# Where the turned probabilities are copied: between the two row maxima on VectorE and between the two exponentials on ScalarE

## The reference, cut to what matters

```python
h = _layernorm(x, axis=-1) * (1 + ca) + sa
q = _l2norm(q) * q_scale          # q, k, v = projections of h, 16 heads of 64
k = _l2norm(k) * k_scale
attn = jnp.einsum('bhid,bhjd->bhij', q, k) * DH ** (-0.5)
attn = jax.nn.softmax(attn, axis=-1)
out = jnp.einsum('bhij,bhjd->bhid', attn, v)
x = x + ga * (out @ Wo.T + bo)    # then layernorm, router, experts
```

## Time and profile before

| | us |
|---|---|
| median of 3 runs | 1300.74 |
| lowest and highest | 1300.59, 1301.45 |
| the profiled execution | 1305.93 |
| its span, first to last instruction | 1304.2 |

### The profile page before, as it was taken

The page is one execution under the profiler, slowest core; times in us unless marked ns, Lnnn a source line. Parts: engine busy times, 40 slices in busy tenths (PEclk is TensorE's granted clock), DMA queues, the critical chain, the costliest instruction groups (busy, mean ns, idle before and its releaser), DMA issues. The chain is left out here.

```text
span 1304.2 us, 28717 instructions
## 1 busy us (share of the span) xinstructions
PE 1240.5 (95%) x9690; PEld 819.9 (63%) x9690; DVE 995.3 (76%) x2049; ACT 967.2 (74%) x2065; POOL 831.5 (64%) x1654
## 2 busy tenths in 40 slices
PE   4899999999999999999999999999998498999997
PEld 4556666666666666666666666666664276788886
DVE  3678778887887887888878878877877776577776
ACT  4677778777778777777778787877775286788886
POOL 2666677767767676777677677866774185344443
PEclk8799999999999999999999999999999699899999
DMA  6000000000000000000000000000000200446441
GB/s 158 2 1 2 1 2 2 2 2 1 2 2 1 2 2 1 2 2 2 2 1 2 2 2 2 1 2 2 1 2 1 67 1 23 102 100 109 100 106 46
DMA packets 36610, 27.99 MB, mean 21 GB/s; under 512 B 8832, under 2 KB 34688, under 8 KB 36480
## 3 DMA queue, kind: packets, MB, share of 16 engines
q1 hardware_dynamic: 35296, 25.92, 8.8%
q10 hardware_dynamic: 1184, 0.40, 0.1%
HBM read 24.09 MB, written 2.23 MB: 20 GB/s over the span
## 5 line engine op out<-in xcount | busy, mean ns | idle before, releaser
L881 ACT ACTIVATE probs<-bank,neg_max 128x512 f32<-128x512 f32 x512 | 347.2, 683 | 216.6 <-DVE neg_max L1013 213.7
L1013 DVE TENSOR_REDUCE neg_max<-bank 128x1 f32<-128x512 f32 x512 | 329.5, 685 | 140.5 <-PE bank L677 138.4
L717 PE MATMUL bank<-probsT,qkv 128*64 128x512 f32 x1024 | 276.8, 620 | 1.3 <-DVE oT L1030 0.8
L677 PE MATMUL bank<-operands 64*128 64x512 f32 x1536 | 249.2, 429 | 2.4 <-ACT probs L881 1.9
L693 PEld LDWEIGHTS T<-ident,probs 64*128 64x128 f32 x4096 | 168.9, 139 | 50.9 <-issue 25.6
L693 PE MATMUL T<-ident,probs 64*128 64x64 f32 x4096 | 172.4, 223 | 5.3 <-issue 3.7
L647 PEld LDWEIGHTS bank<-operands,hT_h 128*128 128x128 f32 x254 | 48.1, 189 | 199.0 <-issue 196.2
L677 PEld LDWEIGHTS bank<-operands 64*128 64x128 f32 x1536 | 125.5, 186 | 64.2 <-issue 42.1
L1197 POOL TENSOR_TENSOR sq<-qkv 128x256 f32<-128x256 f32 x252 | 150.1, 614 | 15.5 <-ACT qkv L860 15.4
L1019 DVE COPY probsT<-T 128x1024 f32<-128x1024 f32 x128 | 155.5, 1215 | 1.5 <-PE T L693 1.5
L1803 POOL TENSOR_TENSOR hid_l<-act_out,hid_h 128x512 fp32r<-128x512 f32 x64 | 83.1, 1298 | 110.0 <-ACT hid_h L1705 110.0
(11 more groups left out here) (259 smaller groups left out, 2371.9 us busy)
## 6 DMA issues: line engine op xcount, KB each, us to landing
probsT<-gate_scratch SPq DMA_DIRECT2D x64, 256.0 KB, 4.7
out<-x_all SPq DMA_DIRECT2D x8, 256.0 KB, 4.6
probsT<-in_L_ffn_fc_w SPq DMA_DIRECT2D x1, 1024.0 KB, 8.9
raw<-in_L_attn_Wq SPq DMA_DIRECT2D x1, 512.0 KB, 4.9
raw<-in_L_attn_Wk SPq DMA_DIRECT2D x1, 512.0 KB, 7.6
raw<-in_L_attn_Wv SPq DMA_DIRECT2D x1, 512.0 KB, 8.8
raw_o<-in_L_attn_Wo SPq DMA_DIRECT2D x1, 512.0 KB, 8.3
route<-in_L_ffn_sh_w SPq DMA_DIRECT2D x2, 256.0 KB, 5.6
```

What stands on the lines that cost most here:

```text
L677: last = nc.tensor.matmul(s_bank(hp, 2 * pair + head)[:], own[rows, q, toks], own[rows, k], start=((q, k) == (QH, KH)), stop=(q == QL))
L717: last = nc.tensor.matmul(O_BANK[rows, :], qkv[:, hp % 4, j, cols], probsT[:, hp % 2, head, j], start=(j == 0), stop=(j == NT - 1), skip_g ...
L881: nc.scalar.activation(probs[:, i % 4], s_bank(hp, i)[:], ACT.Exp, bias=neg_max[:, i:i + 1], accum_out=row_sum[:, hp % 2, i:i + 1]).then_i ...
L1013: nc.vector.reduce_max(neg_max[:, i:i + 1], s_bank(hp, i)[:], AX.X, negate=True).then_inc(max_done, 1)
```

## The change

The same instructions run; two copies in each slot change their place in their engine's order. On VectorE, in pair steps 0 and 2, the copy moves from behind the second maximum (and behind `low_q`) to between the two maxima. On ScalarE, in pair steps 1 and 3, the copy moves from behind the second exponential to between the two exponentials. TensorE's and GpSimd's order is the same.

```diff
@@ ScalarE, slot
                             exponentials(u, hp, 2 * pair)
-                            exponentials(u, hp, 2 * pair + 1)
                             if pair == 1 and earlier >= 1:
                                 copy_transposed(u - 1, hp - 1, 3)
                             if pair == 3:
                                 copy_transposed(u, hp, 1)
+                            exponentials(u, hp, 2 * pair + 1)
@@ VectorE, slot
                             row_max(u, hp, 2 * pair)
+                            if pair == 0 and earlier >= 1:
+                                copy_transposed(u - 1, hp - 1, 2)
+                            if pair == 2:
+                                copy_transposed(u, hp, 0)
                             row_max(u, hp, 2 * pair + 1)
                             if pair == 2 and with_next(b, hp, 1):
                                 low_q(u + 1, hp + 1)
                             if pair == 3 and with_next(b, hp, 1):
                                 low_k(u + 1, hp + 1)
                             if pair == 0 and hp == YT_HP and not is_const(b, 0):
                                 dve.wait_ge(x1_done, b)
-                            if pair == 0 and earlier >= 1:
-                                copy_transposed(u - 1, hp - 1, 2)
-                            if pair == 2:
-                                copy_transposed(u, hp, 0)
```

## The result

The changed kernel takes 1390.37 us (median of 4 runs, 1386.61 to 1392.84) against 1300.81 of before (1300.59 to 1301.45): a ratio of 1.0678, 95% interval 1.0654 to 1.0702, so slower by 6.8%. Its profiled execution took 1388.67 around a span of 1386.8.

The account below looks back on a forecast made before the run. TensorE's own work was taken to bound the slots, so VectorE or ScalarE edits could mainly lose by making it wait. 69.8 + 20.2 + 1 = +91 us on 1300.7 gave 1392, range 1368 to 1404.

Parts of the forecast that it names:

- +1: Behind the last slot: the last exponential comes 0.91 us later and the chain there is serial, +1 us.
- Term one: VectorE, pair step 2: the copy makes `low_q` and the turn of k 1.14 us later in 63 slots, +69.8 us.
- `low_q` without spare time: VectorE to TensorE, pair step 2: `transpose_k` starts 0.12 to 0.15 us behind `low_q`, about the signal between engines.
- The 0.29 that hp 3 had spare: Pair step 2 of hp 3: TensorE turns 0.44 us after `low_q` ends, so 0.29 is spare, 2.0 less in all.
- Term two: ScalarE, pair steps 1 and 3: a unit's last exponential comes 0.91 us later, delaying later scores in some slots, +20.2 us.
- The copy of pair step 0 at nothing: VectorE, pair step 0: the copy delays only the second maximum and its exponential by 1.14 us, no cost by itself.
- tenths that a spare of 1.01 holds: ScalarE, pair steps 0 and 1: later second exponential pushes other work back some tenths, within 1.01 us spare.
- Term one alone: Rival: the delay of the sums' inversion is absorbed, leaving only the pair step 2 loss, 1371 us; chance 8%.
- The copy never waited for the turn: Rival, VectorE pair step 2: the copy waits for TensorE's late turn, adding 13 us, 1405; chance 7%.
- The rival wasn't empty: Rival: TensorE's idle time lowers its granted clock in a tenth of the slots' time, up to +100, 1490 us; chance 4%.

Follow-up runs that it names:

- VectorE's pair step 2 alone: Kernel before with only VectorE's copy of pair step 2 moved between the two maxima: 1370.66 us against 1303.84, ratio 1.0524.
- pair step 3 undone: Changed kernel with ScalarE's copy of pair step 3 put back behind the second exponential: 1371.63 us, ratio 1.0530 to the kernel before.
- three of the runs above: Kernel before with ScalarE's two copies moved, 1324.91 us; changed kernel with VectorE's pair step 2 copy put back, 1326.63, or `low_q` ahead of that copy, 1380.45.
- the kernel with low_q ahead: Changed kernel with `low_q` put between the first maximum and the copy of pair step 2: 1380.45 us against 1304.95 of the kernel before, ratio 1.0585.
- the two runs with low_q ahead: In pair step 2 first maximum, `low_q`, copy, second maximum: in the changed kernel 1380.45 us; in the kernel before, for that step only, 1323.27.
- the split not late: Kernel before with GpSimd's split of an attention output in hp 0 and hp 3 not put behind the squares: span 1306.2 us, single execution.

## Why the prediction was right

**The sum.** Forecast 1392, measured 1390.4. That it is this close is partly luck. In the profiled executions the slots took 85.6 more, where my two terms make 90, and what lies behind the start of the last slot took 313.7 instead of 316.4, where I had counted +1; the spans differ by 82.6, the medians by 89.6. The kernel before ran at 1300.8 beside the changed one and at 1301.8 to 1305.0 beside the other runs. The four runs of the changed kernel go from 1386.6 to 1392.8 as their mean granted clock goes from 0.981 to 0.971. In the profiled one (0.977) batch 2 has the full clock, and the page's slices are below it only at the start and behind the slots; so a few us there are the clock's and not the change's.

**Term one (69.8)** measured 70.4 as a part of its own (VectorE's pair step 2 alone), 66.3 with all but pair step 3 moved, and 68.0 as TensorE's wait in the changed kernel (1.8 before). The step by which it was made, `low_q` without spare time, held in each slot, the same 0.12 behind. The 0.29 that hp 3 had spare came out in the changed kernel (4.78 less 3.90 is 0.88), but it stood on something that I hadn't looked at. TensorE was late in that slot because the turn waited for ScalarE's copy of pair step 1. With that copy moved, the changed kernel's step is 4.78 as in every slot; with it in its old place, VectorE's copy waited for the late turn, and nothing was spare (5.01). In hp 5 I missed as much: its step was 3.87 before and the loss 0.91.

**Term two (20.2)** measured 19.3 (with pair step 3 undone against the changed kernel), 22.8 alone, of which about 1.5 is the fall of the clock. In batch 0 hp 1 to hp 4 lost 1.08, 0.82, 0.92 and 0.83 at pair step 0, where I had 0.91 for each. In a later batch it is 1.9 to 2.1, where I had 2.45. Slot by slot: hp 3 lost 0.80 at pair step 0, as forecast; hp 1 lost 0.40 and 0.30 where I had 0.55 and 0.24; hp 4 lost 0.37 where I had 0.86; hp 5 lost 0.17, for which I had no row. The size of hp 4 is the term's largest error. In the kernel before, timeline of hp 1 and hp 4, GpSimd beside VectorE:

```profile
536.95 1.03 POOL L1213 TENSOR_TENSOR inv_wide<-inv_sum,consts 128x512 f32<-128x512 f32 x1
...
537.67 0.34 DVE L995 TENSOR_SCALAR ss<-ss 128x16 f32<-128x16 f32 x1
...
581.98 1.04 POOL L1213 TENSOR_TENSOR inv_wide<-inv_sum,consts 128x512 f32<-128x512 f32 x1
...
582.39 0.67 DVE L995 TENSOR_SCALAR ss<-ss 128x16 f32<-128x16 f32 x1
...
583.25 1.28 DVE L1013 TENSOR_REDUCE neg_max<-bank 128x1 f32<-128x512 f32 x2
```

The same place, hp 4, in the changed kernel:

```profile
631.28 1.04 POOL L1213 TENSOR_TENSOR inv_wide<-inv_sum,consts 128x512 f32<-128x512 f32 x1 [0.89 <-DVE inv_sum L1024]
...
632.34 0.17 DVE L995 TENSOR_SCALAR ss<-ss 128x16 f32<-128x16 f32 x1
...
632.71 0.69 DVE L1013 TENSOR_REDUCE neg_max<-bank 128x1 f32<-128x512 f32 x1
...
634.26 0.50 PE L677 MATMUL bank<-operands 64*128 64x512 f32 x2 [0.53 <-ACT probs L881]
```

Before, L995 was stretched to end 0.03 to 0.04 after GpSimd's L1213 in both slots (538.01 against 537.98, 583.06 against 583.02). The later inversion of the sums took that overlap away, and VectorE's chain in hp 4 got 0.50 back of the 0.91 it was delayed by, and in hp 1 0.17. That is about what I had too much in each (0.49 and 0.15).

**The copy of pair step 0 at nothing** was right in the changed kernel and wrong by 0.34 in a batch alone, as its run shows; my step "tenths that a spare of 1.01 holds" looked at the scores only and not at the turn, which waits for ScalarE's copy two pair steps on.

**The rivals.** Term one alone (1371) would have been the kernel with pair step 3 undone, 1371.6. The copy never waited for the turn in the changed kernel: it starts 0.60 behind the first maximum (541.03), and the profile's page has 0.0 idle time before L1019. With VectorE's pair step 2 alone it did wait, in hp 3. The clock in the changed kernel's slots stayed at 1.00 from 54 us on, with about 1 us of idle time on TensorE at each turn of k (1.02 in the row above). The Trainium skill ("TensorE: Matmul & The Clock Gate", "Why this matters for your kernels") warns of idle gaps between bursts of matmuls only where they are longer than these, and the trace agrees.

The rival wasn't empty, though, since batch 0 has longer gaps. In three of the runs above the clock fell behind a gap of 2.06 to 2.41 us, and the step took 1.3 to 2.8 us longer than in the kernel before. In the changed kernel it fell for 3.4 us behind a gap of 2.04 that ended at 50.1 us, and didn't behind the one of 2.11 at 93 us. That isn't a loss against the kernel before, which has 11 us at the lower level in that part of batch 0, where the changed kernel has 5. These gaps too are shorter than those in the Trainium skill's warning, so here the measurement decides.

What the prediction didn't have is the kernel with low_q ahead. I thought of term one as the cost of `low_q`'s place alone. It is that in the changed kernel, but the second exponential of pair step 2 is delayed as well. That only the stall at the turn of k hides it, by pausing TensorE, is what the two runs with low_q ahead suggest: they lose time at the later steps once the stall is gone.

## What to carry to other kernels

Price a moved instruction by the results behind it on its engine, and for each by the time between its end and its reader's start less the signal between engines (0.12 to 0.15 us here): where that is zero the whole duration goes onto the critical engine, once in every pass of the loop. Then price the next reader too as if the first wait were gone: two late results can hide behind one stall, and mending the one that the profile names (`low_q`) gave back 4 of 86 us. Spare time is used up once: two delays that cost 2.5 and 2.9 in a batch alone cost 10.2 together. And ask why a reader is late before counting its lateness as spare: with VectorE's copy of pair step 2 moved alone, that copy waited in hp 3 for the same late turn that had made the reader late, and the 0.29 wasn't there.

## What the hardware showed that I had not expected

VectorE's 0.17 us scaling of a 128x16 tile in the state buffer (L995) took 0.34 and 0.67 us when it was due during a GpSimd product of a 128x512 tile, and ended 0.03 to 0.04 after that product both times. The earlier in the product it was due, the longer it took: 0.92 us when it began 0.15 after the product's start (ScalarE's copy of pair step 1 alone). In the changed kernel, with ScalarE's copies alone and with the split not late its longest is 176 to 177 ns. The Trainium skill ("SBUF — State Buffer", "Who interferes with whom") says that VectorE and GpSimd share a port pair that an instruction such as `tensor_scalar` may need, and that whoever has it blocks the other for its whole instruction; these three rows agree. That the port pair is what held L995 is inferred from the matching ends and from the run in which the two don't meet; no run tries it by itself.
